# GpSimd's fetches beside the experts without a wait for the turn of each load

## What is computed

```python
x = x + 0.5 * ffn(layernorm(x))     # 8 experts, top 2, hidden 352, SiLU gate
x = x + attention(layernorm(x))     # 16 heads of 8, no mask
x = x + 0.5 * ffn(layernorm(x))
```

## Time and profile before

| | us |
|---|---|
| median of 3 runs (844.72 to 851.7) | 844.98 |
| the profiled execution | 854.1 |
| its span, first to last instruction | 852.3 |
| mean granted clock of PE, share of full speed | 0.885 |

### The profile page before, as it was taken

How to read it: one execution, slowest core, us unless ns; L and a number is a source line. 1 busy time by engine, 2 the same in 40 slices (tenths; PEclk the granted TensorE clock), 3 DMA queues, 4 the chain that set the end, 5 groups by cost and what they waited for, 6 DMA issues and landing times.

```text
span 852.3 us, 14693 instructions
## 1 busy us (share of the span) xinstructions
PE 651.6 (76%) x4966; PEld 483.1 (57%) x4966; DVE 437.5 (51%) x1115; ACT 395.2 (46%) x926; POOL 302.3 (35%) x311
## 2 busy tenths in 40 slices
PE   4237999999987378887988999676798899889500
PEld 4236888888963134444544554335687788679400
DVE  3724572222345667977988888671457122123211
ACT  0333572433431157756867787583267234234200
POOL 4026543566313243034000000103654345554474
PEclk9999999999995569999989999865899889899855
DMA  6154795777826334244423432015379567567422
GB/s 227 37 182 108 220 265 171 221 204 208 241 88 194 106 99 133 89 131 139 132 88 120 126 107 90 2 57 165 102 216 253 158 187 205 162 194 220 132 77 62
DMA packets 114747, 126.03 MB, mean 148 GB/s; under 512 B 12464, under 2 KB 96944, under 8 KB 114416
## 3 DMA queue, kind: packets, MB, share of 16 engines
q1 hardware_dynamic: 88688, 98.05, 38.2%
q0 software_dynamic: 9088, 18.63, 9.0%
q10 hardware_dynamic: 16896, 8.39, 3.3%
HBM read 89.37 MB, written 35.39 MB: 146 GB/s over the span
## 4 chain that ended last, share of the span: by engine, by line
PE 51%; DVE 19%; issue 10%; ACT 7%; POOL 5%; DMA 3%; another core or an unknown queue 3%; SPq 1%; ACTq 0%; DVEq 0%; POOLq 0%
PE banks L624 10%; PE banks L602 7%; PE banks L607 7%; PE banks L612 7%; DVE mx L917 6%; PE banks L823 6%; POOL rows L541 3%; ACT PT L837 3%; PE banks L753 2%; PE banks L592 2%; PE banks L796 2%; PE banks L462 2%; PE banks L442 2%; ACT oT L890 1%
## 5 line engine op out<-in xcount | busy, mean ns | idle before, releaser
L521 POOL DMA_INDIRECT xe<-routed_rows,idx x156 | 151.7, 972 | 214.9 <-DMA routed_rows<-xn 77.0
L917 DVE TENSOR_REDUCE mx<-banks 128x2 f32<-128x512 f32 x256 | 163.0, 685 | 26.0 <-PE banks L798 20.0
L541 POOL DMA_INDIRECT rows<-slots_out,slot x128 | 123.2, 962 | 106.2 <-ACT PT L837 33.0
L837 ACT ACTIVATE PT<-banks 128x512 f32<-128x512 f32 x256 | 140.3, 602 | 43.3 <-PE banks L809 36.0
L675 DVE TENSOR_TENSOR hidT<-banks,act 96x256 f32<-96x256 f32 (+1 forms) x92 | 34.9, 380 | 237.4 <-ACT act L657 173.0
L624 PE MATMUL banks<-WR,hidT 128*128 128x128 f32 x936 | 121.1, 277 | 5.1 <-ACT ye L665 4.3
L624 PEld LDWEIGHTS banks<-WR,hidT 128*128 128x128 f32 x936 | 113.2, 193 | 8.6 <-issue 6.5
L602 PE MATMUL banks<-xeT,WR 128*128 128x256 f32 (+1 forms) x368 | 93.0, 377 | 22.0 <-issue 20.4
L492 POOL TENSOR_TENSOR rough<-var,half_power 128x16 f32<-128x16 f32 (+1 forms) x8 | 18.4, 2296 | 220.4 <-DVE var L258 220.4
L607 PE MATMUL banks<-xeT,WR 128*96 128x256 f32 (+1 forms) x368 | 89.2, 367 | 6.3 <-DVE hidT L675 6.3
L612 PE MATMUL banks<-xeT,WR 128*128 128x256 f32 (+1 forms) x368 | 87.2, 361 | 0.0
(11 more groups left out here) (155 smaller groups left out, 851.0 us busy)
## 6 DMA issues: line engine op xcount, KB each, us to landing
WR<-in_experts SPq DMA_DIRECT2D x92, 544.0 KB
stacks<-split SPq DMA_DIRECT2D x32, 384.0 KB
slots_out<-ye SPq DMA_DIRECT2D x156, 64.0 KB
routed_rows<-xn ACTq DMA_DIRECT2D x32, 256.0 KB
QS<-stacks SPq DMA_DIRECT2D x64, 112.0 KB
KS<-stacks SPq DMA_DIRECT2D x64, 112.0 KB
xe<-routed_rows,idx POOLq DMA_INDIRECT x156
rows<-in_xt SPq DMA_DIRECT2D x2, 1024.0 KB, 9.4
```

The source lines that it names most:

```text
L521: eng.indirect_dma_start(xe[:, i % XR, a, :], None, routed_rows[h], bass.IndirectOffsetOnAxis(ap=idx[h][:, tile:tile + 1], axis=0))\
L541: eng.indirect_dma_start(rows[:, k, t, :], None, slots_out[h], bass.IndirectOffsetOnAxis(ap=slot[h][:, k, t:t + 1], axis=0))\
L837: eng.activation(PT[:, u % 4, 1 - k].rearrange("p t n -> p (t n)"), PS[f % 3], ACT.Exp, scale=scale).then_inc(s_exp2, 1)
L917: eng.tensor_reduce(mx[:, :, e, pair], MAXIMA[f % 3][:, :].rearrange("p (q n) -> p q n", q=2), AX.X, ALU.max).then_inc(s_max, 1)
```

## The change

The wait at the top of the loop is removed. The gathers, powers and all other waits stay, and their order on GpSimd stays.

```diff
             wanted = KT // 2 if g == 0 else KT
             for i in range(first, first + 2 * NL):
-                wait(eng, s_xt, i + 1)
                 j = i - first
                 if j == 2:
                     root_gpsimd(eng, (1, 7)[g // 2], 1)
```

## The result

The change made the kernel much slower: 992.55 us (median of 4, 991.17 to 993.39) against 845.83 (median of 4), a ratio of 1.172 with a 95% interval of 1.166 to 1.177. The forecast was 846 us. The span of the profiled execution is 991.0 us, 138.7 more than before.

The account below looks back on a forecast made before the run. PE's stream was taken to bound the kernel up to 800 us and GpSimd's after it. The profiled execution came to 854.1 + 1.5 - 0.5 = 855.1 us, the median to 844.98 + 1.0 = 846 us; range 839 to 857.

Parts of the forecast that it names:

- (b): Rest of the first group's gathers in, from 85.5 and 619.8: run without pause, gain 0, transfers cost 1.5 us.
- (d): Gathers out: the first moves from 175.64 to about 171.5, about 4 us likewise in the second stage; wins nothing.
- (a): Start of each expert stage, up to 85.5 and 619.8: nothing moves, 0 us.
- The term for transfers: After 85.5 and 619.8, 7 and 6 more gathers put weight loads back: 0 to 3.5 us, taken as 1.5.
- (c): Gathers in of the next group, after indices at 136.6 and 671.7: issued earlier at 1.25 us each, worth 0.
- (e): End of the second stage: gathers through at about 774, tail unchanged; gain 0 to 1.1 us, taken as 0.5.
- (f): Gathers beside DVE's `hot` operations: GpSimd gives way, DVE loses nothing; GpSimd's 1 us is off the path: 0.
- Denser gathers bring more pauses: Rival, second expert stage: longer runs of back-to-back gathers make PE pause more, 12 us, so 857 us; chance 0.19.
- Its sign: PE idle "issue" or "remote" over 1 us inside 85 to 112, 137 to 163, 619 to 643 or 672 to 698, clock below 1.0.

Follow-up runs that it names:

- the small kernel: Model left out, only handoffs among PE, ACT and DVE, with gathers, loads or other work beside them in stages; 3.45 us a round when nothing disturbs.
- the spaced version: The changed kernel, without the wait, plus a memset of 384 columns behind each gather except in the tail; 825.95 us, 0.975 of the kernel before.
- four kernels with 384 columns: Memset behind gathers: without the wait, loop only, 830.02 us; kernel before with its wait, 829.39; without the wait, all but tail, 829.08, timed again 825.95.

## Why the prediction was wrong

The reading of the bound was right: PE's stream sets the time of the expert stages, and none of GpSimd's waits for turns was on the path. So it was right that nothing could be won by removing one. It was wrong in taking from this that the wait did nothing. It spaced the gathers. The step that failed is (b) to (d): gathers that run on without a pause were charged to the path with 1.5 us of transfers and otherwise with 0, and what they did to the handoffs from PE was put at nothing in the forecast. It was 69.8 us in the first expert stage and 70.0 in the second.

*(a)* "Before these instants nothing moves" held: the first turn is at 60.35 (60.47 before), and the first divergence comes after 85.

*(b)* The gathers did run on at 1.26 us, 21 without a pause being the forecast; 19 went until 109.2, and the last two waited for the ring until 113.47, because PE had stopped. The term for transfers (0 to 3.5 us, taken as 1.5) was the wrong term. The DMA share of the stretch fell to 0.42, and the small kernel shows the hold without any other transfer and none by weight loads alone. The profile also names no wait of PE for weights in the changed kernel. The Trainium skill's rule, from "DMA: Bandwidth & Descriptors" (section on queues, rings and completion order), that DMA engines serve their queues in turn, was taken as a reason for the full 3.5 us and points to the same wrong place; no run showed such a cost.

*(c), (d)* Sizes of what waits on PE's progress all failed with it. Indices came at 162.25 and not at 136.6, 46.6 us after GpSimd had begun to wait for them; the first gather out at 219.26 and not at 171.5, after 21.22 us for the stores. The claim in (d) that GpSimd would wait there and hurt nobody is right: from 192 to 219 PE was busy all the time. Two smaller errors of (c): 23 gathers of the new group stand before the first gather out, not 21, and in the changed kernel the ring did bind, since PE was late (GpSimd waited 3.57 us for a turn until 190.73 and 4.13 until 197.08).

*(e)* Right: the tail from the first gather after the last store to the end is 991.0 - 943.05 = 48.0 us, and was 852.3 - 804.42 = 47.9. The 0.5 us can't be seen in this.

*(f)* Nothing in the runs speaks against it, and it was too small to matter.

*The chances.* "Denser gathers bring more pauses" was the mechanism, named with its place, and given 0.19 and 12 us. Its sign came as written: PE idle "issue" for 2.99 and 11.66 us inside 85 to 112, at a clock of 0.71. Its sum failed in two terms. It counted the dense stretches of the second stage alone, as the first had kept a clock of 0.99; the first lost as much. And it had the rate of loss too low. I took it from a window of the kernel before with 16 gathers in 25 us, 1.56 us each on average, 4.8 us lost in 25, and multiplied it by the longer dense time. But 1.56 us is where the spaced version runs free; at 1.26 us the same PE loses 31 - 14.2 = 16.8 us by standing in 31 us (78 to 109), and by its clock 0.29 x 31 = 9 us counted as the forecast did, or rather 0.29 x 14.2 = 4.1 us, as the clock costs only where PE works. Counted the second way, the three dense windows of the first stage come to 56.1 us of standing and 13.3 by the clock, 69.4 of the 69.8 us (an estimate; what PE stood there before and the window 109 to 116 are left out). A loss that begins at a threshold was treated as proportional. The signs were in the trace: of ACT's 21 "remote" waits of over 1 us, 17 came behind five or more gathers in a row, though not longer behind the longest runs (2.0 and 3.2 us behind 12 and 14 gathers, 5.4 behind 6). I also set against the rival that part of the second stage's 18.2 us might belong to the profiled execution alone. Spacing took 19.5 us off that stage, but the two profiled spans differ by 27.9 us and the medians by 19.5, so a part, of up to 8.4 us over the whole kernel, may have been just that. In the profiles of all four kernels with 384 columns the second stage lasts 187.0 to 190.8 us.

*The range* (839 to 857) let this rival decide with its own price as upper end, and was wrong by 135 us for the same reason.

## What to carry to other kernels

A wait that holds up nothing on the path can still be what paces an engine. Before removing one, ask what rate its engine goes at without it, and whether the trace shows that rate anywhere for long. If ACT, SP and GpSimd start at once after idle time that the profile gives to no one, look at what the remaining engine was doing in a row; here a memset of 0.43 us behind each gather cured it and won 2.5% over the kernel before.

## What the runs showed of the hardware that was not expected

While GpSimd issued indirect gathers faster than one in about 1.5 us, semaphores that PE raised were seen late by ACT, DVE, SP and GpSimd; ACT stood up to 40.7 us. The hold outlasted the run of gathers: the last held raises were seen 4 to 10 us behind it in the small kernel, and some 4 us in this one. PE went on executing what it could. Raises by ACT for PE (PE began 0.36 us behind the start of ACT's copy, in the midst of a pause), by DVE for PE (DVE over at 115.56, PE at 115.61, in the midst of a run of gathers) and between ACT and DVE (1.21 us a round throughout) were not late. Six gathers in a row were free, ten made a round 0.9 us late. 32 rows held as long as 128; plain transfers from GpSimd at 0.53 us each held nothing. For even spacing the limit lay between 1.42 and 1.51 us in the small kernel, between 1.48 and 1.56 in this one.

What piles up, and why PE's raises alone wait for it, stays open: no record of the trace shows it. Nor does the trace tell a late raise from a late completion of PE's last product, since the ends of matmuls are modelled in it. Whether the limit is the same in both kernels is open too: the two ranges overlap. Not tried was whether raises by ACT or DVE would be held if PE's were waiting beside them for longer.
